# Second layer norm's fp16 halves made in phase one and read back transposed by the DMA

## Time and profile before

| | us |
|---|---|
| median of 3 runs | 2360.76 |
| lowest, highest run | 2356.63, 2360.77 |
| span of the profiled execution | 2354.9 |
| its time as a run beside that span | not listed apart; the span is 5.9 under the median |
| PE busy | 2134.7 (91%) |
| DVE busy | 1636.5 (69%) |
| ACT busy | 1198.6 (51%) |
| POOL busy | 909.1 (39%) |
| mean granted TensorE clock | 0.967 |

### The profile page before, as it was taken

One profiled execution on the slowest core, in us unless ns is written; L12 is line 12 of the kernel. 1 busy time (PEld: TensorE's weight loads), 2 busy tenths in 40 slices (PEclk: granted clock), 3 DMA queues, 4 the chain that ended last, 5 costly groups with the idle time before them and its releaser, 6 DMA issues. The chain is left out here.

```text
span 2354.9 us, 38531 instructions
## 1 busy us (share of the span) xinstructions
PE 2134.7 (91%) x10581; PEld 1058.4 (45%) x10581; DVE 1636.5 (69%) x3637; ACT 1198.6 (51%) x2482; POOL 909.1 (39%) x1126
## 2 busy tenths in 40 slices
PE   5999999999999999999999999965888887888985
PEld 2445555445555444555544555532333333433432
DVE  6745656664654774565666465577999999999994
ACT  3443323444333344332344433234888888878876
POOL 1102211201211210211120021124899989998998
PEclk9999999999999999999999999996999999999998
DMA  4101112100111210111210011122322222222232
GB/s 144 54 23 48 56 39 84 53 32 30 61 47 54 73 54 23 43 52 48 74 62 32 25 55 59 54 77 95 90 85 84 82 85 89 77 88 87 76 94 76
DMA packets 91009, 151.20 MB, mean 64 GB/s; under 512 B 9538, under 2 KB 27074, under 8 KB 90820
## 3 DMA queue, kind: packets, MB, share of 16 engines
q1 hardware_dynamic: 90820, 149.05, 19.7%
HBM read 86.36 MB, written 62.65 MB: 63 GB/s over the span
## 5 line engine op out<-in xcount | busy, mean ns | idle before, releaser
L453 PE MATMUL psum<-v,work 128*128 128x512 f16 x1632 | 371.5, 379 | 1.2 <-DVE work L709 0.8
L453 PE MATMUL psum<-kT,qT 128*128 128x512 f16 (+3 forms) x1920 | 362.8, 347 | 0.0
L453 PE MATMUL psum<-work,w_hi 128*128 128x512 f16 x1024 | 309.6, 384 | 11.5 <-ACT xcT L628 7.5
L590 ACT ACTIVATE work<-psum 128x512 f16<-128x512 f32 (+2 forms) x228 | 125.3, 552 | 341.3 <-PE psum L537 298.2
L943 POOL TENSOR_SCALAR ve<-mv 128x1 f32<-128x1 f32 x66 | 14.7, 223 | 691.9 <-DVE mv L768 691.9
L453 PEld LDWEIGHTS psum<-kT,qT 128*128 128x128 f16 x1920 | 181.0, 98 | 171.1
L709 DVE SCALAR_TENSOR_TENSOR work<-psum,work 128x512 f16<-128x512 f32 (+2 forms) x228 | 143.3, 628 | 152.9 <-ACT work L590 150.3
L1326 DVE MAX8 c<-cut 128x8 f32<-128x512 f32 x384 | 243.9, 675 | 0.0
L453 PEld LDWEIGHTS psum<-v,work 128*128 128x128 f16 x1632 | 158.6, 98 | 171.1 <-DVE work L709 4.1
L1110 PE MATMUL psum<-fw,xsT 128*128 128x512 f16 x792 | 208.8, 420 | 1.1 <-ACT xsT L1212 1.1
L453 PE MATMUL psum<-work,w_lo 128*128 128x512 f16 x512 | 196.5, 384 | 0.0
(11 more groups left out here) (147 smaller groups left out, 4283.1 us busy)
## 6 DMA issues: line engine op xcount, KB each, us to landing
work<-x SPq DMA_DIRECT2D x72, 256.0 KB, 3.1
out<-zn SPq DMA_DIRECT2D x70, 256.0 KB, 3.0
h_scratch<-hb SPq DMA_DIRECT2D x68, 256.0 KB, 2.3
x<-x_scratch SPq DMA_DIRECT2D x66, 256.0 KB, 2.8
x_scratch<-xr SPq DMA_DIRECT2D x65, 256.0 KB, 2.1
h<-h_scratch SPq DMA_DIRECT2D x65, 256.0 KB, 3.7
xr<-x SPq DMA_DIRECT2D x64, 256.0 KB, 2.7
xc_scratch<-xcT SPq DMA_DIRECT2D x68, 128.0 KB, 2.1
```

The lines of the kernel that those rows point to most:

```text
L453: mm = nc.tensor.matmul(outp, stat(a), mov(c), start=(n == 0 and k == 0), stop=(n == total - 1 and k == 2))
L590: nc.scalar.activation(dst, src, ACT.Copy, scale=scale).then_inc(t_hi.sem, 1)
```

## The change

Phase one gets a buffer hhl (two slots of two halves, 128x512 fp16). After the second norm of a tile ACT writes its high half, scaled by 256 (`hi_h2`), DVE the low half (`lo_h2`), and SP stores both as one 256 KB transfer to a new DRAM tensor, hl_scratch (`store_hl`). In phase two PE's four transposes and `less_hi` for h2, and ACT's two `half` on HT_BANK, are gone. In their place SP issues per tile two transposing loads of 128x512 fp16 (`load_hT`), which write h2T directly; h2T has four buffers in place of two. h2 in fp32 is still stored and loaded.

```diff
+        hl_d = nc.dram_tensor("hl_scratch", [(B + 1) * TILES, 2, P, D], F16, kind="Internal").ap()
+            hhl = sa("hhl", [P, 2, 2, D], F16)
-            h2T = sc("h2T", [P, 2, 2, C, P], F16)
+            h2T = sc("h2T", [P, 4, 2, C, P], F16)
...
+                def store_hl(b, t):
+                    sp.wait_ge(hhl_lo.sem, hhl_lo.at(b, t))
+                    sp.dma_start(hl_d[bass.ds(b * TILES + (TILES + t), 1)].rearrange("o h p n -> p (o h) n"), hhl[:, t % 2]) \
+                        .then_inc(hl_out[t % 2].sem, 16)
...
                     if g < 3:
                         store_h2(b, g - 3)
+                        store_hl(b, g - 3)
...
                             store_h2(b, i - 6)
+                            store_hl(b, i - 6)
...
+                def hi_h2(b, t):
+
+                    act.wait_ge(h2_ok.sem, h2_ok.at(b, t))
+                    act.wait_ge(hl_out[t % 2].sem, hl_out[t % 2].at(b, t // 2 - 1))
+                    nc.scalar.activation(hhl[:, t % 2, 0, :], hb[:, t % 2, :], ACT.Copy, scale=W_SCALE).then_inc(hhl_hi.sem, 1)
...
                             hi_v(b, GROUP * g + j)
+                        if g < 3:
+                            hi_h2(b, g - 3)
                         conv_out(b, g - 4)
...
                             conv_out(b, i - 7)
+                        if 0 <= i - 6 < TILES:
+                            hi_h2(b, i - 6)
...
+                    dve.wait_ge(hhl_lo.sem, hhl_lo.at(b, t - 2))
...
+                def lo_h2(b, t):
+
+                    dve.wait_ge(hhl_hi.sem, hhl_hi.at(b, t))
+                    nc.vector.scalar_tensor_tensor(hhl[:, t % 2, 1, :], hb[:, t % 2, :], W_SCALE, hhl[:, t % 2, 0, :], ALU.mult,
+                                                   ALU.subtract).then_inc(hhl_lo.sem, 1)
...
                         lo_v(b, GROUP * g + GROUP - 1)
+                        if g < 3:
+                            lo_h2(b, g - 3)
...
                             conv_stats(b, i - 8)
+                        if 0 <= i - 6 < TILES:
+                            lo_h2(b, i - 6)
                 for g in range(GROUPS):
                     late_tiles(B, g)
+                    if g < 3:
+                        lo_h2(B, g - 3)
...
-                for a in (yT, ob, xr, hb, xcs, xcT, mv2, mv3, rs2, rs3):
+                for a in (yT, ob, xr, hb, hhl, xcs, xcT, mv2, mv3, rs2, rs3):
...
                 def load_h2(r, n):
                     sp.wait_ge(xs_ok.sem, xs_ok.at(r, n - 4))
-                    sp.wait_ge(hT_ps.sem, hT_ps.at(r, n - 4))
...
+                def load_hT(r, n):
+                    sp.wait_ge(full_ps.sem, full_ps.at(r, n - 4))
+                    pair = hl_d[bass.ds(tile_row(r, n) + TILES, 1)]
+                    for a in range(2):
+                        sp.dma_start_transpose(h2T[:, n % 4, a], pair[:, a].rearrange("o p n -> (o p) n")) \
+                            .then_inc(hT_in[n % 4].sem, 16)
...
                         load_h2(r, n + 1)
+                        load_hT(r, n + 1)
                         load_x1(r, n - 2)
                         store(r, n - LAG_OUT)
...
                     if not tail:
                         logits(r, n + 1)
-                        pe.wait_ge(h2_in[n % 4].sem, h2_in[n % 4].at(r, n // 4))
-                        pe.wait_ge(hT_lo.sem, hT_lo.at(r, n - 1))
-                        transposed(h2[:, n % 4, :], HT_BANK, hT_ps)
                     m = n - 1
                     if due(1):
-                        pe.wait_ge(hT_lo.sem, hT_lo.at(r, m))
+                        pe.wait_ge(hT_in[m % 4].sem, hT_in[m % 4].at(r, m // 4))
                         pe.wait_ge(tf_ok.sem, tf_ok.at(r, m - 2))
-                        product(F_BANK[m % 2], h2T[:, m % 2], full_ps)
-                    if not tail:
-                        pe.wait_ge(hT_hi.sem, hT_hi.at(r, n))
-                        less_hi(HT_BANK, h2T[:, n % 2, 0], hm_ps)
+                        product(F_BANK[m % 2], h2T[:, m % 4], full_ps)
...
-                    if not tail:
-                        half(r, n, hT_ps, HT_BANK, h2T[:, n % 2, 0], hT_hi)
...
-                    if not tail:
-                        half(r, n, hm_ps, HT_BANK, h2T[:, n % 2, 1], hT_lo)
```

More of the change, by code:

```diff
@@ L265, in layer_block @@
         h2_out = [sig(f"h2_out{j}", TILES // 2, late=1 + j, step=16) for j in range(2)]
+        hl_out = [sig(f"hl_out{j}", TILES // 2, late=1 + j, step=16) for j in range(2)]
         xc_out = [sig(f"xc_out{j}", TILES // 2, late=2, step=16) for j in range(2)]
@@ L303, in layer_block @@
         h2_ok = sig("h2_ok", TILES, late=3)
+        hhl_hi = sig("hhl_hi", TILES, late=3)
+        hhl_lo = sig("hhl_lo", TILES, late=3)
         pr_ok = sig("pr_ok", 2 * TILES, late=6)
@@ L439, in _ @@
                     sp.wait_ge(s.sem, s.at(B, 1))
-                for s in x1_out + h2_out + xc_out:
+                for s in x1_out + h2_out + hl_out + xc_out:
                     sp.wait_ge(s.sem, s.at(B, -1))
@@ L691, in _ @@
                 for g in range(GROUPS):
+                    if g < 3:
+                        hi_h2(B, g - 3)
                     conv_out(B, g - 4)
@@ L1005, in layer_block @@
         xs_ok = sig_b("xs_ok", SIDE, late=1)
-        hT_ps = sig_b("hT_ps", SIDE)
-        hT_hi = sig_b("hT_hi", SIDE)
-        hm_ps = sig_b("hm_ps", SIDE)
-        hT_lo = sig_b("hT_lo", SIDE)
+        hT_in = [sig_b(f"hT_in{n}", SIDE // 4, step=32) for n in range(4)]
         xT_ps = sig_b("xT_ps", SIDE, late=1)
@@ L1029, in layer_block @@
         signals_b = {
-            "sp": xc_in + h2_in + x1_in + out_st,
-            "pe": [lg_ps, hT_ps, hm_ps, xT_ps, xm_ps, full_ps, in_ps],
-            "act": [gelu_ok, xa_hi, nmx_ok, e8_ok, ex_ok, hT_hi, hT_lo, xT_hi, xT_lo, tf_ok, tin_ok, zsum_ok,
+            "sp": xc_in + h2_in + hT_in + x1_in + out_st,
+            "pe": [lg_ps, xT_ps, xm_ps, full_ps, in_ps],
+            "act": [gelu_ok, xa_hi, nmx_ok, e8_ok, ex_ok, xT_hi, xT_lo, tf_ok, tin_ok, zsum_ok,
                     zneg_ok, zsq_ok, zn_ok],
@@ L1037, in layer_block @@
         L_BANK = [psum[:, n, :] for n in (0, 1)]
-        HT_BANK, XT_BANK = psum[:, 2, :], psum[:, 3, :]
+        XT_BANK = psum[:, 3, :]
         F_BANK = [psum[:, n, :] for n in (4, 5)]
@@ L1082, in _ @@
                 load_h2(0, 0)
+                load_hT(0, 0)
                 sp.wait_ge(setup_b["pool"], 6)
@@ L1097, in _ @@
                 sp.wait_ge(h2_in[0].sem, h2_in[0].at(R, 0))
+                sp.wait_ge(hT_in[0].sem, hT_in[0].at(R, 0))
                 for s in out_st:
@@ L1288, in _ @@
                 i.then_inc(setup_b["dve"], 1)
-                for a in (ex[:, 3], rest[:, 1], h2T[:, 1], xsT[:, 0], zn[:, 0]):
+                for a in (ex[:, 3], rest[:, 1], h2T[:, 3], xsT[:, 0], zn[:, 0]):
                     nc.vector.memset(a, 0.0)
```

9 lines of the change are left out of this document (5 added, 4 removed).

## The result

The changed kernel takes 2371.23 us (median of 4 runs, 2365.96 to 2373.91); the kernel before, beside it, 2360.77 us (2356.63 to 2361.77). The ratio is 1.0050, 95% interval 1.0037 to 1.0064: slower by 10.5 us. 2373.7 was forecast. The same kernel run again (e10) was slower by 7.9 us, ratio 1.0029. The forecast was 2.5 us too high, but mostly because two errors cancelled.

What follows compares the result with a forecast made beforehand. PE was taken to bound phase one, DVE phase two. Terms 1.8 + 6.4 + 2.2 + 3.8 + 2.0 - 3.3 = +12.9 on the 2354.9 us span, plus 5.9 around it, gave 2373.7; 8-in-10 range 2357 to 2397.

Steps and rivals of the forecast that it cites:

- start: Start of phase one: POOL clears one more buffer, nothing covers it, PE's first transpose comes later; +1.8 us.
- groups 0 and 1: Phase one: load_x queues behind the halves' store, which waits for lo_h2; 0.8 us stall at eight places, +6.4 (0 to 16).
- steps 6 to 15: Phase one: hi_h2 and lo_h2 end each step, but PE has queued scores and ACT and DVE catch up; nothing.
- "step 16": Phase one: no scores left, PE already waited 1.17 us for yT's low half, ACT's copy comes ahead; 4 x 0.55 = +2.2.
- turns to the next batch: Phase one: two lo_h2 and their hi_h2 precede a norm PE already waits for; 3 x 1.25 = +3.8 (1 to 6).
- end of phase one: Last tiles: three lo_h2 in a chain with no PE work left, plus the last turn; +2.0 us (0.6 to 4).
- the terms around the DMA: Phase two: a transposing pair takes 5.2 us a tile, fits in 7.9 of room, costs nothing; phase one's extra stores cost nothing.
- the 5.9 us around the span: Whole kernel: the median of the runs lies 5.9 us above the profiled span, added to 2367.8 to give 2373.7.
- A: Rival: transposing loads bound phase two from 7.9 us a tile; +365 us, about 2739, at the upper bound; chance 0.15.
- B: Rival: DVE's 25.9 us of phase-two gaps are waits for ACT; 29.2 us gained, 2347.8, faster; chance 0.08.
- C: Rival: phase one hides everything, late loads fit in the slack and only the start stays; about 2361; chance 0.12.
- D: Rival: with less work PE stays at half clock, 1.2 GHz, in phase two; +160 us, about 2520; chance 0.03.

Runs made afterwards that it cites:

- e10: The changed kernel run again, nothing changed: 2365.37 us, 1.0029 to the kernel before.
- e6: Changed kernel without the two instructions making the halves (zeros stored and loaded), plus 19 one-element DVE memsets ahead of its phase-two loop: 2346.01 us, 0.9951 to the kernel before.
- e5: Kernel before with only 19 one-element memsets added on DVE ahead of its phase-two loop: 2348.82 us, 0.9958 to the kernel before.
- e1: Phase one as in the changed kernel (halves made and stored, nobody reads them), phase two as in the kernel before: 2369.48 us, 1.0039 to the kernel before.
- e7: Kernel before with only 38 one-element memsets added on DVE ahead of its phase-two loop: 2347.11 us, 0.9952 to the kernel before.
- e8: Changed kernel with each pair of transposing loads issued four times, three into a spare buffer: 2480.78 us, 1.0519 to the kernel before.
- e2: Changed kernel without hi_h2 and lo_h2; a cleared buffer is stored, stores and transposing loads stay: 2363.15 us, 1.0022 to the kernel before.
- e4: Changed kernel with the halves made a step later, their store behind the loads of x, no memset of hhl: 2357.17 us, 0.9991 to the kernel before.

## Why the prediction was right, and where it was not

**Right:** the sign, its cause (phase one pays, because PE is its bound and the added work reaches it), and that what is taken from PE and ACT in phase two is worth next to nothing, since DVE sets the time there. e6 against e5 puts the last at 0.2 us of phase two, and so does the changed kernel against e1; the forecast had 3.3, the sum of DVE's waits for ACT, in a range from 0 to 5. In the changed kernel those waits did fall, from 3.3 to 0.6 us. PE's freed time went into waiting: for POOL's xs it waits 104.0 us of phase two, before 43.4, and 52.7 for ACT's half. That the time came within 2.5 us of the forecast is luck.

**Wrong: "The change doesn't touch DVE's loop in phase two."** It does not touch its instructions, but it moves them. The forecast read the 14 gaps rightly as the turn of the loop's own code, saw two parts in them, 2.30 and 1.5, and let both stay. The second was a matter of place, and the 19 instructions put in ahead of the loop took it away: -10.9. This is the step that failed, and it pulled the result towards faster. The prediction's own sign of being wrong, a passage under 86 us, came true with 85.8, and its sign of being right, gaps of 3.8 us a turn, did not.

**Wrong in size: phase one, +24.5 for +16.2.** Term by term, from how far PE's transposes and the matmuls behind them stand behind their fellows of before, in this pair of profiles and between the means of the four profiles with the changed phase one and the five with the old:

| term | forecast | this pair | means |
|---|---|---|---|
| start | 1.8 | 1.5 | 1.1 |
| groups 0 and 1 | 6.4 | 4.0 | 4.4 |
| steps 6 to 15 | 0 | 0.9 | 0.9 |
| "step 16" | 2.2 | 6.6 | 6.6 |
| rest of step 17 | 0 | 1.7 | 3.3 |
| turns to the next batch | 3.8 | 6.2 | 2.9 |
| end of phase one | 2.0 | 3.5 | 3.2 |

- *Start.* PE's first transpose began at 20.51 in place of 19.40 (21.2 was forecast); in the three other profiles with this phase one it began at 16.4 to 20.7. POOL's memset of hhl took 1.81 us, as taken.

- *Groups.* The mechanism is as described: load_x behind the halves' store, which waits for lo_h2. In group 0 of the second batch the load went out at 464.94, 12.1 us later than before; 8.0 of it is the lag of the whole phase by then (SP's store of h2 just ahead went out at 460.17, before at 452.19), the other 4.1 is the wait for the store of the halves. DVE then stood 3.51 us for the data:

```profile
463.41 0.68 DVE L817 SCALAR_TENSOR_TENSOR hhl<-hb,hhl 128x512 f16<-128x512 f32 x1
467.61 0.69 DVE L743 BATCH_NORM_STATS2 st<-work 128x6 f32<-128x512 f32 x1 [3.51 <-DMA work<-x]
```

  PE's stalls for it were 0 to 1.3 us, half a microsecond in the mean, where 0.8 was taken.
- *"Step 16".* The largest miss, and a misread place. The transposition that already waited 1.17 us belongs to step 17, and there are two exposed steps, 16 and 17, and not one. Where no scores are left to cover them, PE lost 0.81 and 0.85 us, 1.66 a batch and not 0.55, in each of the four batches. The stall itself:

```profile
403.04 0.65 PE L500 MATMUL psum<-idn,work 128*128 128x128 f32 x4 [2.02 <-DVE yT L734]
436.84 1.11 PE L500 MATMUL psum<-idn,work 128*128 128x128 f32 x4 [2.36 <-DVE work L750]
```

- *Turns.* The second row is the turn to the next batch: 1.00 before, 2.36 now; the three turns cost 2.9, 4.0 and -0.6 us. But a turn varies by itself: from the last transpose of step 17 to the last of group 0 it takes 31.4 to 35.1 us in the five profiles with the old phase one. In e7's longest PE waits 3.48 us for the normed tile. The mean, 2.9, is near the forecast.
- *Rest of step 17.* In the last batch of the changed kernel the stretch behind the stall took 5.34 us, in the others 3.66, with the same 2.02 us of waiting before it. The granted clock was lower, 0.68 in place of 1.00:

```profile
1572.58:1577.92 5.34, 5.34 (x20) 2.79 (x21) 4.34 (x8) 1.19 (x2) 1.09 (x3) 0.68 0.62 206
```

  In the four profiles with the changed phase one this happened eight times in 16 batches, in those with the old one never in 20.
- *End.* 3.5 us in the last tiles.

The pattern in it: wherever cover had already run out, the forecast counted the added instruction once (0.55 to 1.25 us). The runs show the chain ACT's half, DVE's wait for it, DVE's half, in a place where DVE waited 1.5 us in the mean. This and the stalled steps that it took for one are the terms that were mis-sized.

**Wrong: the terms around the DMA.** The pair of transposing loads was taken at 5.2 us of the 16 engines a tile. The pages' rows of q1 give the price. After, then e1, which has the stores but no transposing load, then e8:

```profile
q1 hardware_dynamic: 180036, 183.93, 27.9%
```

```profile
q1 hardware_dynamic: 109316, 166.88, 22.1%
```

```profile
q1 hardware_dynamic: 392196, 235.10, 36.2%
```

By subtraction, 27.9% of 2364.2 less 22.1% of 2368.6 is 136 us for 130 loads: 1.05 us each, 2.1 us a pair. They take (180036 - 109316) / 130 = 544 packets each, as guessed (512 a load), but at 31 ns a packet in place of 82. From after to e8, 237 us for 390 more loads, it is 0.61. The 68 plain stores of 256 KB that e1 has over the kernel before cost 0.87 us each in the same way, so the pair takes over twice as long for as many bytes. Nothing followed for the sum, since the term was zero either way. What the prediction left out is the SP queue: two of these issues take 2.52 us a tile of it.

```profile
1907.70 2.52 SPq L1105 DMA_TRANSPOSE h2T<-hl_scratch  x2
```

That was free here, because SP waits most of the time (L1110, 403.3 us in phase two). Of the two statements of the Trainium skill that the prediction weighed, 1309 ns a block ("VectorE: DVE Perf Modes", The three transpose paths), an estimate of 10.5 us for eight in a row, does not add up over a tile: the pair took 2.1 us of the engines. The Trainium skill's other statement, that transposing DMAs are as fast as regular ones ("Advanced Engine Details and Errata", X-Bar Transpose (TRN2)), holds for the landing only in part, since a load of h2 in fp32, twice the bytes of one transposing load, lands in the same 4.1 us; and not for the time of the engines, 2.1 us against 0.87.

```profile
h2T<-hl_scratch SPq DMA_TRANSPOSE x130, 4.1
h<-h_scratch SPq DMA_DIRECT2D x65, 256.0 KB, 4.1
```

**Wrong: the 5.9 us around the span.** The profiled run of the kernel before took 2356.63 us, its lowest, 1.7 over its span; the changed kernel's 2365.96, 1.8 over. So 1.7 lies around the span and 4.1 was the distance of that run from the median. The changed kernel's profiled run was its fastest too, so that its median lies 7.0 over its span, where 5.9 was taken.

**The rivals.** A (the loads become the bound): refuted, no wait of PE for them is in the changed kernel's phase two; e8 shows that at four times their number it is SP's queue that gives in, before the engines. B (the gaps are waits for ACT): 10.9 of its 25.9 us did go, but its cause was wrong: with ACT's work back in e1 the gaps stay away, and without it in e2 they are there. C (phase one hides all): refuted, +24.5. D: refuted for phase two; the passage's clock is 0.92 against 0.94, and DVE's pace did not follow it. In phase one a slower clock did cost something, in the step 17 above.

**The sum, as the runs have it.** Phase one +24.5 (+22.4 in the mean, 18 to 26), the place of the code -10.9, true waits for ACT and the tail -4. Against a kernel before that has its code in a good place too, e5, the change stands worse: ratios of 1.0050 (1.0029 in e10) and 0.9958 to the same kernel, 0.7 to 0.9% or 17 to 22 us slower (the ratios were not taken on one chip). The best version is the kernel before with 19 or 38 idle memsets, 0.9958 and 0.9952. A changed kernel with the halves out of PE's way (e4) came to 0.9991.

What stays open: which of the added instructions' waits would have to go for the steps to lose their 7.5 us, why the clock falls in some step 17s and not in others after the same wait, and why a turn takes 31.4 us in one run and 35.1 in another of the same code.

## What to carry to other kernels

In a profile, idle time marked as issue at a hardware loop's turn is a cost of its own and hangs on where the code lies: before crediting or blaming an edit for a few microseconds, look whether such gaps came or went, and try a few idle instructions ahead of the loop. Work taken from engines beside the bound is worth only the bound's true waits for them; work added beside a bound engine is hidden only where that engine has queued work at that very moment, so look at the steps with none, and count the whole chain that is put there, not the last instruction.

## What the runs showed that I had not expected

- Code position: seven turns of a loop cost 25.9 us of DVE's time or 15, by the place of its first instruction alone, with blocks of 128 instructions: seven gaps fewer are seven packets fewer in the instruction queue. A second gap is 1.5 us in the kernel before and up to 3.1 in e2, which has more DMA traffic.
- A transposing load of 128x512 fp16 takes 1.26 us of the issuing queue, 544 packets and 0.6 to 1.05 us of all 16 DMA engines. Eight a tile with the other loads are bound by the queue at 12.3 to 13.1 us a tile, with the engines at 0.71.
- The same code varies in its turns: a turn between batches took 31.4 to 35.1 us in five profiles with one phase one, and the aggregates differ by 4 us.
